# Cross-attention and a routed expert layer on one core: routing counts in rows with two stages less, the last output projection in three parts, and the first pair's second layer moved up

## The reference

```python
x = x + (softmax(causal(mask(q(layernorm(x)) @ k(ctx).T / 8))) @ v(ctx)) @ Wo + bo
xn = layernorm(x).reshape(8192, 256)
e = argmax(xn @ router_w.T + router_b)             # one expert of 32 for each token
h = relu(xn @ weights1[e] + bias1[e])              # 256 -> 64
x = x + relu(h @ weights2[e] + bias2[e])           # 64 -> 256
```

## Time and profile before

| what | value |
|---|---|
| time, median of 3 runs | 1553.86 us (1553.06 to 1555.27) |
| time of the profiled execution | 1550.49 us |
| its span, first to last instruction | 1548.8 us |
| PE busy | 1484.6 us (96%) |
| DVE busy | 1228.4 us (79%) |
| ACT busy | 1013.5 us (65%) |
| POOL busy | 360.9 us (23%) |
| mean granted TensorE clock | 0.982 of full |

### The profile page before, as it was taken

One profiled execution on the slowest core, in us unless ns is written; L12 is line 12 of the kernel. 1 busy time (PEld: TensorE's weight loads), 2 busy tenths in 40 slices (PEclk: granted clock), 3 DMA queues, 4 the chain that ended last, 5 costly groups with the idle time before them and its releaser, 6 DMA issues.

```text
span 1548.8 us, 44990 instructions
## 1 busy us (share of the span) xinstructions
PE 1484.6 (96%) x14149; PEld 1280.5 (83%) x14150; DVE 1228.4 (79%) x5089; ACT 1013.5 (65%) x3145; POOL 360.9 (23%) x507
## 2 busy tenths in 40 slices
PE   8999999999999999999999999999999999678787
PEld 7888888888888888888888888888888888546554
DVE  5888888888898888888888888889888888554443
ACT  5766776677666766777667666766676667334443
POOL 3111212222221121211122222222212111125555
PEclk9999999999999999999999999999999999888998
DMA  8543000000000000000000000000000000044431
GB/s 281 125 147 112 28 28 28 22 26 28 28 28 21 28 28 27 23 28 21 28 28 28 28 26 23 28 28 28 22 27 28 28 15 14 15 124 152 146 111 25
DMA packets 70405, 77.77 MB, mean 50 GB/s; under 512 B 11351, under 2 KB 64221, under 8 KB 70369
## 3 DMA queue, kind: packets, MB, share of 16 engines
q1 hardware_dynamic: 62546, 60.37, 13.7%
q0 software_dynamic: 7680, 16.93, 3.0%
q10 hardware_dynamic: 144, 0.03, 0.0%
HBM read 47.61 MB, written 33.88 MB: 53 GB/s over the span
## 4 chain that ended last, share of the span: by engine, by line
PE 88%; DVE 4%; another core or an unknown queue 2%; issue 2%; ACT 1%; DMA 1%; DVEq 1%; POOL 1%; ACTq 0%; SPq 0%; POOLq 0%
PE psR L513 35%; PE psS L583 14%; PE psO L649 12%; PE psR L545 12%; PE psR L628 6%; PE psS L1465 2%; PE psR L504 2%; PE psR L555 2%; PE psR L1455 1%; PE psR L1452 1%; DVE XH L1344 1%; DVEq L1295 1%; PE psO L1443 1%; PE psR L1443 1%
## 5 line engine op out<-in xcount | busy, mean ns | idle before, releaser
L788 ACT ACTIVATE Sm<-Sm,mneg 128x128 f32<-128x128 f32 (+1 forms) x1024 | 453.4, 456 | 153.5 <-DVE mneg L1086 153.5
L1086 DVE CUSTOM_DVE_ANT_0 Sm<-psS,MK 128x128 f32<-128x128 f32 (+1 forms) x1024 | 303.8, 354 | 4.0 <-PE psS L583 1.4
L781 ACT ACTIVATE PT<-psR 128x512 f32<-128x512 f32 x384 | 201.6, 598 | 134.0 <-PE psR L628 130.1
L583 PE MATMUL psS<-KT,QT 64*128 64x128 f32 (+1 forms) x2048 | 250.7, 355 | 5.4 <-DVE V L763 2.4
L788 ACT ACTIVATION_READ_ACCUMULATOR Sm<-Sm,mneg 128x1 f32 x1024 | 205.0, 200 | 0.0
L649 PE MATMUL psO<-PT,V 128*64 128x256 f32 (+1 forms) x2048 | 196.0, 334 | 0.6 <-DVE OT_lo L1106 0.3
L1101 DVE SCALAR_TENSOR_TENSOR Sm<-Sm,halve,rinv 128x512 f32<-128x512 f32 x256 | 191.4, 748 | 0.0
L583 PEld LDWEIGHTS psS<-KT,QT 64*128 64x128 f32 x2048 | 148.2, 187 | 30.7 <-issue 7.2
L649 PEld LDWEIGHTS psO<-PT,V 128*64 128x64 f32 x2048 | 127.4, 137 | 49.1 <-DVE OT_lo L1106 1.9
L628 PEld LDWEIGHTS psR<-ident,Sm 64*128 64x128 f32 x3072 | 143.9, 139 | 21.0 <-DVE Sm L1101 2.5
L1092 DVE RECIPROCAL rinv<-rsum 128x4 f32<-128x4 f32 x256 | 44.2, 173 | 133.5 <-ACT Sm L788 130.2
(11 more groups left out here) (156 smaller groups left out, 3130.7 us busy)
## 6 DMA issues: line engine op xcount, KB each, us to landing
lists<-pad SPq DMA_DIRECT2D x8, 1560.0 KB, 10.5
XS<-lists SPq DMA_DIRECT2D x48, 260.0 KB
x_in<-in_x SPq DMA_DIRECT2D x32, 256.0 KB, 3.1
ctx_in<-in_ctx SPq DMA_DIRECT2D x32, 256.0 KB, 2.7
xr<-in_x SPq DMA_DIRECT2D x32, 256.0 KB, 2.6
W2R<-in_L_ffn_weights SPq DMA_DIRECT2D x1, 2048.0 KB
out<-Y,tok POOLq DMA_INDIRECT x96
W2R<-in_L_xattn_Wv SPq DMA_DIRECT2D x2, 512.0 KB, 9.6
```

The source lines that it names most:

```text
L583: last = nc.tensor.matmul(psS[:, 2 * i + side, o:o + (it + 1) * P], QT[rows, p, it * P:(it + 1) * P], KT[rows, p, 0:(it + 1) * P], start=T ...
L781: nc.scalar.activation(PT[:, s % 2, 512 * k:512 * k + 512], psR[:, k, :], ACT.Copy).then_inc(s_pt, 1)
L788: nc.scalar.activation(v, v, ACT.Exp, bias=mneg[:, s % 2, k:k + 1], scale=-1.0, accum_out=rsum[:, s % 2, k:k + 1]).then_inc(s_exp, 1)
L1086: nc.vector.tensor_tensor_reduce(out=Sm[:, 2 * (s % 2) + i, side, cols], in0=psS[:, 2 * i + side, cols], in1=MK[:, cols], scale=-SCALE, sc ...
```

## The change

Three edits:

- **Routing.** The counts of fresh tiles are kept in rows instead of in tiles: over and more_t are 128 or 0 each, both computed from upto_now in one stage. The running sum adds both inputs, so the all-zero tile zeros_e goes. last_t is now over + more_t. fresh comes out in rows at once, because taken starts at -128. The stages `tiles_more` and `rows_next` are gone; the copy of taken and the comparison below (now against first_row, 128 times the partition number less 128) move to `rows_gap`. jump gets its mask in `row_places`, and the sum mine is taken there too, both behind place and ahead of the signal that lrow waits for. The number of DVE operations from `counted` to `fills` is 24 before and after; the waits on `s_rk` in a batch go from 9 to 7.
- **Wo of the last batch** is issued as pairs 0 to 3, then (behind `values`) 4 and 5, then 6 and 7, each with its own wait on `s_o`. Before, 4 to 7 was one part.
- **The first expert pair.** PE runs y_of(0) directly behind hid(0), ahead of turn(2) and hid(1).

```diff
-            nc.gpsimd.memset(taken[:], 0.0).then_inc(s_const, 1)
+            nc.gpsimd.memset(taken[:], -float(P)).then_inc(s_const, 1)
...
             wo(B - 1, psR[:, 0, :], range(0, 4))
             values(B - 1, QUADS - 1)
-            wo(B - 1, psR[:, 0, :], range(4, PAIRS))
+            wo(B - 1, psR[:, 0, :], range(4, 6))
+            wo(B - 1, psR[:, 0, :], range(6, PAIRS))
...
             def tiles_over(b):
                 dve.wait_ge(s_rk, CH * b + 1)
-                nc.vector.tensor_scalar(over[:], upto_now[:], float(P), None, ALU.is_gt).then_inc(s_rk, 1)
-
-            def tiles_more(b):
-                dve.wait_ge(s_rk, CH * b + 2)
-                nc.vector.scalar_tensor_tensor(out=more_t[:], in0=upto_now[:], scalar=float(2 * P), in1=over[:],
-                                               op0=ALU.is_gt, op1=ALU.add).then_inc(s_rk, 1)
+                nc.vector.tensor_scalar(over[:], upto_now[:], float(P), float(P), ALU.is_gt, ALU.mult)
+                nc.vector.tensor_scalar(more_t[:], upto_now[:], float(2 * P), float(P), ALU.is_gt, ALU.mult
+                                        ).then_inc(s_rk, 1)
 
             def tiles_run(b):
-                wait_apart(dve, s_passed, s_rk, CH * b + 3)
-                nc.vector.tensor_tensor_scan(run_t[:], more_t[:], zeros_e[:], 0.0, ALU.add, ALU.add).then_inc(s_rk, 1)
+                wait_apart(dve, s_passed, s_rk, CH * b + 2)
+                nc.vector.tensor_tensor_scan(run_t[:], over[:], more_t[:], 0.0, ALU.add, ALU.add)
+                nc.vector.tensor_tensor(last_t[:], over[:], more_t[:], ALU.add).then_inc(s_rk, 1)
...
             def row_places(b):
                 dve.wait_ge(s_lr, 2 * b + 1)
-                nc.vector.tensor_reduce(place[:], far[:], AX.X, ALU.add).then_inc(s_lr, 1)
+                nc.vector.tensor_reduce(place[:], far[:], AX.X, ALU.add)
+                nc.vector.scalar_tensor_tensor(out=jump[:], in0=over[:], scalar=0.0, in1=jump[:], op0=ALU.is_gt, op1=ALU.mult)
+                nc.vector.tensor_reduce(mine[:], below[:], AX.X, ALU.add).then_inc(s_lr, 1)
...
                 def pairs_of(i, first, more):
                     for u in range(U):
+                        if first and u == 0:
+                            y_of(i, u, False)
...
-                        y_of(i, u, not first or u >= 2)
+                        if not first or u > 0:
+                            y_of(i, u, not first or u >= 2)
```

More of the change, by code:

```diff
@@ L125, in attention_moe @@
         mine = sb("mine", [P, 1])
-        zeros_e = sb("zeros_e", [P, E])
+        first_row = sb("first_row", [P, 1])
         pad = sb("pad", [P, ROW])
@@ L416, in _ @@
             nc.gpsimd.memset(cur[:], 0.0).then_inc(s_const, 1)
-            nc.gpsimd.memset(taken[:], 0.0).then_inc(s_const, 1)
+            nc.gpsimd.memset(taken[:], -float(P)).then_inc(s_const, 1)
             nc.gpsimd.memset(owner[:], 0.0).then_inc(s_const, 1)
-            nc.gpsimd.memset(zeros_e[:], 0.0).then_inc(s_const, 1)
+            nc.gpsimd.iota(first_row[:], [[1, 1]], base=-P, channel_multiplier=P,
+                           allow_small_or_imprecise_dtypes=True).then_inc(s_const, 1)
             nc.gpsimd.iota(iota_e[:], [[1, E]], base=0, channel_multiplier=0,
@@ L973, in one_hot @@
                                         ).then_inc(s_oh, 1)
-            CH = 9
+            CH = 7
             def counted(b):
@@ L999, in tiles_next @@
+                nc.vector.tensor_tensor(last_t[:], over[:], more_t[:], ALU.add).then_inc(s_rk, 1)
             def tiles_next(b):
-                dve.wait_ge(s_rk, CH * b + 4)
[L1001 to L1009, removed]
@@ L1011, in rows_gap @@
-            def rows_gap(b):
-                dve.wait_ge(s_rk, CH * b + 6)
+                dve.wait_ge(s_rk, CH * b + 3)
+                nc.vector.scalar_tensor_tensor(out=fresh[:], in0=run_t[:], scalar=taken[:, 0:1], in1=last_t[:],
+                                               op0=ALU.add, op1=ALU.subtract)
+                nc.vector.tensor_scalar(nxt_t[:], run_t[:], taken[:, 0:1], None, ALU.add).then_inc(s_rk, 1)
+            def rows_gap(b):
+                dve.wait_ge(s_rk, CH * b + 4)
@@ L1013, in rows_gap @@
                 nc.vector.tensor_tensor(run_t[:], cur[:], fresh[:], ALU.subtract)
                 nc.vector.tensor_tensor(far[:], rank[:], fresh[:].unsqueeze(1).broadcast_to([P, TT, E]), ALU.add)
-                nc.vector.scalar_tensor_tensor(out=last_t[:], in0=more_t[:], scalar=float(P), in1=fresh[:],
-                                               op0=ALU.mult, op1=ALU.add)
-                nc.vector.tensor_reduce(mine[:], below[:], AX.X, ALU.add).then_inc(s_rk, 1)
+                nc.vector.tensor_copy(taken[:], nxt_t[:, E - 1:E])
@@ L1019, in rows_near @@
+                nc.vector.tensor_scalar(below[:], nxt_t[:], first_row[:, 0:1], None, ALU.is_le).then_inc(s_rk, 1)
             def rows_near(b):
-                dve.wait_ge(s_rk, CH * b + 7)
+                dve.wait_ge(s_rk, CH * b + 5)
                 nc.vector.scalar_tensor_tensor(out=rank[:], in0=rank[:], scalar=float(P),
@@ L1023, in rows_near @@
                                                op0=ALU.is_lt, op1=ALU.mult)
-                nc.vector.tensor_tensor(jump[:], last_t[:], cur[:], ALU.subtract).then_inc(s_rk, 1)
+                nc.vector.tensor_tensor(jump[:], last_t[:], fresh[:], ALU.add).then_inc(s_rk, 1)
             def rows_all(b):
-                dve.wait_ge(s_rk, CH * b + 8)
+                dve.wait_ge(s_rk, CH * b + 6)
                 nc.vector.tensor_tensor(far[:], far[:], rank[:], ALU.add)
-                nc.vector.tensor_tensor(jump[:], jump[:], over[:], ALU.mult).then_inc(s_rk, 1)
+                nc.vector.tensor_tensor(jump[:], jump[:], cur[:], ALU.subtract).then_inc(s_rk, 1)
             def rows_kept(b):
-                dve.wait_ge(s_rk, CH * b + 9)
+                dve.wait_ge(s_rk, CH * b + 7)
                 nc.vector.tensor_tensor(far[:], far[:], OH[:], ALU.mult).then_inc(s_lr, 1)
@@ L1044, in fills @@
                 nc.vector.tensor_tensor(cur[:], cur[:], jump[:], ALU.add)
-                nc.vector.scalar_tensor_tensor(out=fill[:], in0=more_t[:], scalar=-float(P), in1=upto_now[:],
-                                               op0=ALU.mult, op1=ALU.add)
+                nc.vector.tensor_tensor(fill[:], upto_now[:], last_t[:], ALU.subtract)
                 nc.vector.tensor_tensor(owner[:], owner[:], mine[:], ALU.add).then_inc(s_own, 1)
             ROUTER_END = (rows_gap, rows_near, rows_all, rows_kept, row_places, row_numbers, fills)
-            ROUTER = (largest, where_largest, expert_ids, one_hot, counted, tiles_over, tiles_more, tiles_run,
-                      tiles_next, rows_next) + ROUTER_END
+            ROUTER = (largest, where_largest, expert_ids, one_hot, counted, tiles_over, tiles_run,
+                      tiles_next) + ROUTER_END
             def first_key(b):
@@ L1211, in iteration @@
                         route(prev, b - 1, tiles_over)
-                        route(prev, b - 1, tiles_more)
                         norm(1)
```

1 line of the change is left out of this document (removed).

## The result

| | median | runs |
|---|---|---|
| before | 1554.01 us | 6 (1553.06 to 1556.08) |
| changed kernel | 1560.84 us | 6 (1559.29 to 1566.43) |

The ratio is 1.0043, with a 95% interval of 1.003 to 1.0056: 6.8 us slower, between 4.7 and 8.7. That is outside of the predicted range, whose upper end was 1557.0.

A forecast was written before the change was run, and what follows sets the result against it. PE was taken to bound the loop, with engines waiting for each other in the second block. Terms -0.25 - 0.25 + 0.15 + 0.5 = +0.15 us gave 1550.6 for the profiled execution, 1554.0 us for the median; range 1550.5 to 1557.0.

The forecast's parts named there:

- Routing, in the loop: Routing in each loop batch: any DVE saving is covered by busy PE, so 0.
- Routing, last batch and batch 30: Routing chain to lrow in the last batch and in batch 30: shorter, -0.25 us each.
- Wo in three parts: End of attention: wo ends earlier, but the residual waits for the scatter's landing, so 0.
- Transposes at half clock: Last batch's transposes: PE idles earlier, so all run at half clock, +0.15 us, bounds 0 and 0.3.
- The first pair: Start of the second block: first Y slightly earlier, second y_of 1.3 us late; +0.5 us, bounds -0.3 and +1.5.
- The rounds of the second block break up: Rival, POOL's scatter rounds in the second block: several rounds with one pair alone, slower, 1558 us, chance 0.15.
- The last pairs keep the full clock: Rival, end of the second block: full clock kept, -4 to -6 us, 1549.5 us, chance 0.12.
- If DVE's chain counted in each batch: Rival, the loop: DVE's shorter chain gains in each batch, -14 us, 1540 us, chance 0.02.

The follow-up runs named there:

- e4: Changed kernel with all three edits, but jump's mask and mine moved behind lrow with their own signal: 1552.59 us, ratio 1.0012 to the kernel before.
- e1: Kernel before with the routing edit alone: 1558.89 us, ratio 1.005, period 41.43 us.
- e6: Kernel before with two extra small DVE reductions, read by nobody, directly ahead of place: 1512.76 us (1 run) against 1507.20, period 41.42 us.
- e7: Kernel before with four extra small DVE reductions, read by nobody, directly ahead of place: 1519.11 us (1 run) against 1507.20, period 41.61 us.
- e12: Kernel before with OT_lo of step 0 ahead of place instead of behind it: 1555.68 us (1 run) against 1555.08, period 41.33 us.
- e3: Kernel before with Wo of the last batch in three parts alone: 1551.18 us, ratio 1.0004.
- e2: Kernel before with the first pair's y_of(0) moved ahead alone: 1553.88 us, ratio 1.0013.
- e10: Kernel before with six dummy matmuls on PE behind y_of(0), order unchanged: 1555.47 us, ratio 1.0006.
- e11: The changed kernel measured again, on one chip with the kernel before: 1561.25 us, ratio 1.0041.
- e5: Changed kernel with jump and mine behind lrow and the old first-pair order: 1506.27 us, ratio 0.9996 to the kernel before.
- e8: Kernel before with y_of(0) behind turn(2), ahead of hid(1) only: 1507.94 us, ratio 1.0009.

## Why the prediction was wrong

**Routing, in the loop: 0. This step failed.** It said that "whatever it saves on DVE is covered by PE, busy 299.92 of 300 us". That is right for what is *saved*: e4 has the saving and gains nothing. But the step looked only at the sum of the operations, 24 and 24. It never asked what stands behind each operation that moves. jump and mine went from stages with slack into `row_places`, and the next instruction on DVE is the one that PE waits for. It measured +0.16 us a batch, 4.5 us in all in the two traces (e1, e4, e6 and e7 show the cause). The kernel before showed the risk: OT_lo ended at 527.46 and `wo` began at 527.63, directly behind the transposes. There were some 0.03 us to spare, and the change put 0.19 ahead. The busy share could not show it; it reads 299.88 with the wait in it, and only with e7's double wait does it fall, to 299.03. Nor was it so that "PE waits for nothing": in each batch of the kernel before, the weight loads idle for 0.07 us at the scores that wait for DVE's residual (see e12).

**Routing, last batch and batch 30: -0.25 each. Right.** Over to lrow fell by 0.27 us. For batch 30 lrow came 3.78 us behind upto_now instead of 4.05, again 0.27. Whether the residual came sooner by it can't be seen: from lrow to the residual it is 6.1 us before and 5.5 after, and 4.9 to 6.4 over all traces.

**Wo in three parts: 0. Right.** The scatter still releases the residual, `wo` is done 1.76 us ahead, and e3 is 1.0004. The cover was thin, though: with `wo` in two parts the residual started between 0.94 us (kernel before) and 0.04 us (e12) behind the end of `wo`, and in e12 the profile names `wo` as its releaser.

**Transposes at half clock: +0.15. Right in this pair of traces,** with 1.11 us instead of 1.06: +0.19. The granted clock there was 0.50. But that the change makes it isn't shown. The five traces with `wo` in three parts all have 1.11 us, and those with two parts have 0.83 to 1.12, four of them 1.11 or 1.12 (e2, e6, e10, e12).

**The first pair: +0.5, bounds -0.3 and +1.5. Sign likely right, size not settled.** The hole (1.44 us for "about 1.5") and the first round with pair 0 alone came as described; the second y_of came 1.5 us later behind hid(0) than before, for 1.3. The third Y came 1.0 us sooner, not later, counted from the first XH (1388.68 - 1375.52 = 13.16, before 1383.59 - 1369.43 = 14.16), but in e11, the same kernel, it came at 15.72. It was no good sign to go by. The runs of the edit give +0.6 to +2.0.

**The rivals.** "The rounds of the second block break up" had the sign and nearly the time (1558), for another reason: one short round came at the start, and the two others early in the block stand in the trace of the kernel before too. The short round lasted 4.4 us here and 5.7 in e11. The prediction's 5.0 counts the 0.30 us between two issues once too often: 1.28 + 0.97 + 2.45 is 4.7. "The last pairs keep the full clock" didn't happen: the clock fell again near the end (0.70 in 1530 to 1535 us, 0.84 in 1545 to 1550). "If DVE's chain counted in each batch" had the right place and the wrong sign: it was thought of only as a gain, and given 0.02.

The sum by what was measured: 4.5 - 0.27 - 0.27 + 0.19 + (0.6 to 2.0) = 4.8 to 6.2 us, against 6.8 (4.7 to 8.7) and 6.4 (4.4 to 8.4). e1 alone, at 7.8 (4.7 to 10.9), is above its own sum of 4.0. What is shown is the loop's part: taken alone (e1), taken away (e4), and in doses (e6, e7). The first pair's part, +0.6 to +2.0 us, is likely and not shown.

## What to carry to other kernels

When an operation moves in an in-order stream, look at the next instruction behind its new place that another engine waits for; equal counts say nothing. Keep updates of state behind the signal that others need. And judge a loop by the distance between the same instruction in two iterations and by the idle time of the weight loads, since a busy share of 99.9% can hide a wait of 0.16 us in 41.

## What was not expected of the hardware

**The second block runs at another pace on another chip.** The kernel before took 1551.06, 1554.01 and 1555.08 us on three occasions, and 1507.20 (21 runs) on the chip of e5 to e8. The difference lies in the second block: e5's last OH is at 1358.0 us, that of the kernel before in the other chip's trace at 1357.7. e5's scatters by tile, and the first and the third of three in the timeline:

```profile
L1303 POOL DMA_INDIRECT out<-Y,tok x96: 972/976/1128, 1379.0 to 1501.9; - x96
```

```profile
1400.76 0.98 POOL L1303 DMA_INDIRECT out<-Y,tok  x1 [0.30 <-issue]
...
1403.32 0.98 POOL L1303 DMA_INDIRECT out<-Y,tok  x1 [0.30 <-issue]
```

Two of them every 2.56 us, without a round, where the kernel before stops for 2.4 us after four. An issue itself takes as long (976 ns against 973). The stretch 1400 to 1500 us, first of e5 and then of the kernel before in its own trace:

```profile
1400.00:1500.00 100.00, 95.55 (x668) 72.37 (x666) 60.61 (x182) 60.14 (x148) 75.52 (x78) 1.00 0.50 149
```

```profile
1400.00:1500.00 100.00, 82.74 (x505) 58.30 (x504) 44.05 (x140) 46.72 (x115) 55.58 (x58) 0.91 0.46 143
```

PE does a pair each 2.55 us there and has its full clock, where before it idled for 17% of the stretch at a mean clock of 0.91. So the rounds, and the waits whose releaser the profile doesn't know, don't come from the program alone. The kernel before has no trace of its own on that chip; its median says the same. What makes the rounds on the other chips was not tested.
